# Inputs laid out ahead of the kernel and a new order of its instructions, in an attention and mixture-of-experts kernel

## The reference

```python
logits = jnp.einsum('bhqd,bhkd->bhqk', Q, K) + b[0]
logits = logits + -1e+30 * (1.0 - mask)
weights = jax.nn.softmax(logits, axis=-1)
out = jnp.einsum('bhqk,bhkd->bhqd', weights, V)
```

## Time and profile before

| what | value |
|---|---|
| median of three runs | 539.66 us |
| the profiled execution, its own time | 538.97 us |
| its span, first to last instruction | 537.2 us |
| mean granted TensorE clock | 0.982 |
| TensorE busy | 497.7 us (93%) |
| VectorE busy | 433.1 us (81%) |
| GpSimd busy | 364.5 us (68%) |
| ScalarE busy | 356.7 us (66%) |

### The profile page before, as it was taken

One profiled execution on the slowest core, in us unless ns is written; L12 is line 12 of the kernel. 1 busy time (PEld: TensorE's weight loads), 2 busy tenths in 40 slices (PEclk: granted clock), 3 DMA queues, 4 the chain that ended last, 5 costly groups with the idle time before them and its releaser, 6 DMA issues.

```text
span 537.2 us, 15110 instructions
## 1 busy us (share of the span) xinstructions
PE 497.7 (93%) x5549; PEld 324.0 (60%) x5549; DVE 433.1 (81%) x1404; ACT 356.7 (66%) x761; POOL 364.5 (68%) x633
## 2 busy tenths in 40 slices
PE   1756999999999999999999999999999999999893
PEld 1645565666656565766666566666666666655551
DVE  4735868899897979888897979799887785867897
ACT  3398698887967867677686866777566665655410
POOL 7644444588858869686868778686845857654865
PEclk9987899999999999999999999999999999999997
DMA  7402101010310101010110101000000000100010
GB/s 170 101 4 55 32 16 56 2 51 6 82 36 18 34 22 51 23 50 21 31 43 21 52 1 51 21 21 27 3 21 1 2 22 1 33 1 21 1 31 29
DMA packets 28503, 16.98 MB, mean 32 GB/s; under 512 B 3687, under 2 KB 28429, under 8 KB 28430
## 3 DMA queue, kind: packets, MB, share of 16 engines
q1 hardware_dynamic: 26670, 15.57, 10.5%
q10 hardware_dynamic: 1760, 0.46, 0.4%
HBM read 11.74 MB, written 4.24 MB: 30 GB/s over the span
## 4 chain that ended last, share of the span: by engine, by line
PE 64%; DVE 5%; issue 1%; ACT 0%; DVEq 0%
PE ps L2186 16%; PE ps L2134 16%; PE ps L2145 4%; PE ps L2079 4%; PE ps L2022 4%; PE ps L2096 4%; PE ps L2127 4%; PE ps L2164 2%; PE ps L2165 2%; PE ps L2104 2%; PE ps L2054 2%; PE ps L2177 2%; DVE weighed L1046 1%; PE ps L2083 1%; PE ps L2047 1%
## 5 line engine op out<-in xcount | busy, mean ns | idle before, releaser
L2186 PE MATMUL ps<-w_moeT,y4T 128*128 128x512 f32 x256 | 123.5, 607 | 1.2 <-DVE gd L1005 1.1
L613 POOL TENSOR_TENSOR sum<-weighed 128x512 f32<-128x512 f32 x60 | 76.1, 1269 | 71.2 <-DVE weighed L1046 71.2
L2134 PE MATMUL ps<-h,w 128*128 128x512 f16 x512 | 118.6, 379 | 0.0
L1638 ACT ACTIVATE h<-ps 128x512 f16<-128x512 f32 x128 | 74.1, 591 | 46.9 <-PE ps L2134 35.9
L1046 DVE TENSOR_TENSOR weighed<-ps,wgt 128x1024 f32<-128x1024 f32 x64 | 77.8, 1218 | 31.7 <-PE ps L2186 30.7
L969 DVE SCALAR_TENSOR_TENSOR h<-ps,h 128x512 f16<-128x512 f32 x128 | 85.6, 682 | 20.2 <-ACT h L1638 20.1
L2134 PEld LDWEIGHTS ps<-h,w 128*128 128x128 f16 x512 | 48.3, 98 | 56.2 <-issue 5.6
L1604 ACT ACTIVATE prT<-ps,maskT 77x1024 f32<-77x1024 f32 x64 | 67.3, 1101 | 14.8 <-PE ps L2083 14.5
L2186 PEld LDWEIGHTS ps<-w_moeT,y4T 128*128 128x128 f32 x256 | 45.1, 189 | 43.0 <-issue 35.0
L565 POOL TENSOR_TENSOR rs<-ve,neg_half 128x4 f32<-128x4 f32 x64 | 64.9, 1013 | 8.7
L560 POOL TENSOR_TENSOR ve<-mv,eps 128x4 f32<-128x4 f32 x64 | 14.2, 222 | 60.6 <-DVE mv L903 60.4
(11 more groups left out here) (171 smaller groups left out, 986.1 us busy)
## 6 DMA issues: line engine op xcount, KB each, us to landing
cx<-in_ctx SPq DMA_DIRECT2D x16, 308.0 KB
xa<-in_x SPq DMA_DIRECT2D x16, 256.0 KB, 3.0
out_x<-xo SPq DMA_DIRECT2D x16, 256.0 KB, 2.3
plugs<-plug_d SPq DMA_DIRECT2D x16, 77.0 KB
nat<-in_L_ffn_W SPq DMA_DIRECT2D x1, 512.0 KB
k_u<-in_L_ffn_k ACTq DMA_DIRECT2D x1, 256.0 KB, 3.9
k_u<-in_L_ffn_k ACTq DMA_DIRECT2D x1, 128.0 KB, 3.4
k_u<-in_L_ffn_k ACTq DMA_DIRECT2D x1, 64.0 KB, 4.6
```

The costliest lines, as they stand in the source:

```text
L613: nc.gpsimd.tensor_tensor(sum4[:], both[:, 0:4 * D], both[:, 4 * D:8 * D], ALU.add).then_inc(c_sum4.sem, 1)
L1638: last = nc.scalar.activation(h[:, 0, (k - 1) % FC, :], src, ACT.Relu)
L2134: last = pe.matmul(pb(g, k), w2[:, i, c * 128:(c + 1) * 128], h1[:, g.p, part, i, :], start=(i == 0 and part == 0), stop=(i == FC - 1 and ...
L2186: last = pe.matmul(pm(g, j)[:, half, :], y4T[:, g.p, j * S:(j + 1) * S], w_moeT[:, half * 512:(half + 1) * 512], start=True, stop=True)
```

## The change

The order of the calls is new on all five engines, and the host-side function `kernel()` lays the inputs out before the launch, in a new function `laid_out`: only reshapes, transposes, copies, zeros and ones. The kernel's own arithmetic stays on the chip.

- The keys arrive turned and already spread with zeros for every other head (`kT`, 308 KB a group), the values with their column of ones (`vx`, 308 KB a group). `a_turn_keys`, `a_keys`, `a_values_in` and `make_values` are gone. The context is still loaded for the patches. `x` and the output are arranged so that each partition has one contiguous row of 2 KB a group.
- The experts' weights, `W_in` and the gate arrive turned, in one tile, with a second copy that repeats the last row; GpSimd subtracts it in place (`make_sums_zero`). `turn_weights`, `take_weights` and the turn of the mask are gone; the turned mask is loaded.
- The Boolean inputs come in one transfer and the scales in another, issued by ScalarE after `a_normalise(g[0])`. `make_weights` moves from ScalarE to VectorE.
- Two of the mask's four rows are sent from ScalarE's queue, ahead of its first work.
- The normalisations of groups 1 to 3 in stage a, and half of the third norm of group 15, are on VectorE.
- The sums at the end: group 14 has j = 1 and 3, group 15 j = 2 and 3 on VectorE, now as eight dependent multiply-and-add steps of 128 columns straight from PSUM (`e_accumulate`); group 15's j = 1 is weighed by ScalarE and summed by nine matmuls with the unit matrix (`e_sum`), and copied out (`e_take`). `keep_busy` is gone.

```diff
 SyncE:
             def load_keys(g):
+                if g.has(2):
+                    sp.wait_ge(a_less[1].sem, a_less[1].of(g, back=2))
+                sp.dma_start(kT[:, g.p], keys[g.n]).then_inc(keys_in[g.p].sem, 16)
+            def load_values(g):
+                if g.has(2):
+                    sp.wait_ge(a_pv.sem, a_pv.of(g, back=2))
+                sp.dma_start(vx[:, g.p], values[g.n]).then_inc(values_in[g.p].sem, 16)
...
             def mask_rows():
                 sp.wait_ge(made_mask, 1)
-                for r in range(R):
+                for r in range(R // 2):
                     sp.dma_start(mask_b[32 * r:32 * r + 1, :], mask0_b[:]).then_inc(masks_in, 16)
...
             load_rows(g[0])
-            load_masks()
+            load_mask()
+            load_lens()
+            load_context(g[0])
             load_rows(g[1])
             load_keys(g[0])
             mask_rows()
+            load_context(g[1])
+            load_values(g[0])
             load_keys(g[1])
...
+            load_values(g[14])
+            load_keys(g[14])
+            store(g[8])
+            load_values(g[15])
+            store(g[9])
+            plug(g[13])
             load_keys(g[15])
 VectorE:
+            def make_weights():
+                dve.wait_ge(made_s, 6)
+                dve.wait_ge(made_halves, 1)
+                nc.vector.tensor_scalar(w1[:], k0_d[:], s_sgn[:, 7:8], None, ALU.mult)
+                nc.vector.tensor_scalar(w2[:], k1_u[:], s_sgn[:, 5:6], s_sgn[:, 6:7], ALU.mult, ALU.add)
+                nc.vector.tensor_scalar(w3[:], k2_u[:], 2.0, -1.0, ALU.mult, ALU.add).then_inc(made_ffn, 1)
...
+            def a_normalise(g):
+                dve.wait_ge(ln_a.rs.sem, ln_a.rs.of(g))
...
+                for j in range(G):
+                    last = nc.vector.tensor_scalar(xn[0][:, g.p, j * D:(j + 1) * D], xa[:, g.f, j * D:(j + 1) * D],
+                                                   mv[0][:, g.p, j, 0:1], rs[0][:, g.p, j:j + 1], ALU.subtract, ALU.mult)
+                last.then_inc(a_xn_v.sem, 1)
...
+            def e_accumulate(g, j, half):
...
+                for e in range(4 * half, 4 * half + 4):
+                    so_far = xo if e else xd
+                    if e:
+                        dve.wait_ge(v_step.sem, v_steps(g, j) + e)
+                    last = nc.vector.scalar_tensor_tensor(xo[:, g.p, cols], pm(g, j)[:, e // 4, (e % 4) * D:(e % 4 + 1) * D],
+                                                          wgt[:, g.p, j, e:e + 1], so_far[:, g.p, cols], ALU.mult, ALU.add)
+                    last.then_inc(v_step.sem if e < E - 1 else c_weighed.sem, 1)
...
+            a_highest(g[1], 0)
+            make_weights()
+            a_stats(g[2])
+            make_plug()
+            a_stats(g[3])
+            a_highest(g[1], 1)
+            a_normalise(g[2])
+            a_split_maxima(g[1])
+            a_normalise(g[3])
             a_weigh(g[0])
...
+            e_weigh(g[15], 0)
+            e_accumulate(g[15], 2, 0)
+            e_accumulate(g[15], 2, 1)
+            e_accumulate(g[15], 3, 0)
+            e_accumulate(g[15], 3, 1)
 ScalarE:
+            def mask_rows():
+                act.wait_ge(made_mask, 1)
+                for r in range(R // 2, R):
+                    act.dma_start(mask_b[32 * r:32 * r + 1, :], mask0_b[:]).then_inc(masks_in, 16)
...
+            def e_weigh(g, j):
...
+                for e in range(E):
+                    last = nc.scalar.activation(weighed[:, place(g, j), e * D:(e + 1) * D],
+                                                pm(g, j)[:, e // 4, (e % 4) * D:(e % 4 + 1) * D], ACT.Copy,
+                                                scale=wgt[:, g.p, j, e:e + 1])
+                last.then_inc(s_weighed.sem, 1)
...
+            mask_rows()
+            a_normalise(g[0])
             load_signs()
-            a_normalise(g[0])
-            a_keys(g[0])
             a_queries(g[0])
...
             a_exponent(g[1], 0)
+            b_normalise(g[0])
+            a_exponent(g[1], 1)
+            b_high(g[0], 0)
 TensorE:
+            def e_sum(g, j, *readers):
...
+                for e in range(E):
+                    pe.matmul(dst, ident[:], weighed[:, place(g, j), e * D:(e + 1) * D], start=(e == 0), stop=False)
+                pe.matmul(dst, ident[:], xd[:, g.p, j * D:(j + 1) * D], start=False, stop=True).then_inc(s_sum.sem, 1)
...
-            a_turn_keys(g[0])
             turn_ends()
             a_turn_rows(g[0])
             a_scores(g[0], 0)
+            a_turn_rows(g[1])
+            a_scores(g[0], 1, (a_max[0], g[0]))
             count_ends((s_ends, g[0]))
...
             a_scores(g[2], 1, (a_max[0], g[2]))
             b_turns(g[0], (a_prT[1], g[1]))
...
+            e_experts(g[13], 1, (a_prT[1], g[15]))
+            b_last(g[15])
             e_experts(g[13], 2, (c_weighed, g[13], 1))
-            b_last(g[15])
```

```diff
             e_experts(g[7], 2, (c_weighed, g[7], 2))
-            a_turn_rows(g[12], (a_prT[1], g[10]))
             a_turn_out(g[10])
             b_layer(g[9], 3)
             c_turns(g[8], (c_weighed, g[7], 3))
+            a_turn_rows(g[12], (a_prT[1], g[10]))
             b_layer(g[9], 4)
             a_turn_maxima(g[11], (a_att, g[10]))
-            a_turn_keys(g[12])
             c_project(g[8])
             a_scores(g[12], 0, (a_mT, g[11]))
             b_layer(g[9], 5)
+            e_experts(g[7], 3, (c_x3, g[8]), (c_yT, g[8]))
             b_layer(g[9], 6)
-            e_experts(g[7], 3, (c_x3, g[8]), (c_yT, g[8]))
```

More of the change, by code:

```diff
@@ L60, in turned_at, with build @@
         return self.turned.of(g, self.k, back)
[L63 to L68, removed]
-    G = 4
-    NG = B // G
+def build(nc, x, ctx, keys, values, mask, mask_turned, lens, b_attn, signs, scales, weights, biases, gains, patch_gains, out):
+    B, NK = mask.shape
+    G = 4
+    NG, S, D = x.shape[0], x.shape[1], x.shape[2] // G
+    DC = ctx.shape[2] // G
+    FC = 4
+    F = FC * D
+    assert signs.shape[1] == (2 + FC) * F + FC * D
+    E = weights.shape[2] // D - 1
     HD = D // HEADS
@@ new lines, in count, with place, place_free @@
+        def count(kind, g, j):
+            return sum(1 for i, k in sums_of if how(i)[k] in kind and (i.n, k) <= (g.n, j))
+        def place(g, j):
+            return buffered.index((g.n, j)) % 2
+        def place_free(g, j):
+            n, k = buffered[buffered.index((g.n, j)) - 2]
+            if how(Group(n))[k] == "scalar":
+                return s_sum.sem, s_sum.of(Group(n), k + 1)
+            return c_sum4.sem, added(Group(n), k)
+        def added(g, j):
+            return count(("gpsimd",), g, j)
@@ new lines, in v_steps, with __init__, of @@
+        def v_steps(g, j):
+            return (count(("vector",), g, j) - 1) * (E - 1)
+        class Counted(Signal):
+            def __init__(self, sem, kinds):
+                self.sem, self.kinds = sem, kinds
+            def of(self, g, k=None, back=0):
+                return count(self.kinds, Group(g.n - back), (G if k is None else k) - 1)
+        c_weighed = Counted(c_weighed.sem, ("gpsimd", "vector"))
+        s_weighed, s_sum, s_out = [Counted(s.sem, ("scalar",)) for s in (s_weighed, s_sum, s_out)]
@@ L360, in bcast, with shared, by_vector, normalised @@
+        def shared(ln, g):
+            return g.n == NG - 1 and ln.n == 2
+        def by_vector(ln, g):
+            return ln.n == 0 and 1 <= g.n <= 3
+        def normalised(ln, g, back=0):
+            i = Group(g.n - back)
+            if by_vector(ln, i):
+                return a_xn_v.sem, i.n
+            return ln.xn.sem, i.n + 1 - (3 if ln.n == 0 and i.n > 3 else 0)
         def bcast(ap, n):
@@ new lines, in normalise_rest @@
+            def normalise_rest(ln, g, src):
+                n, p = ln.n, g.p
+                dve.wait_ge(ln.rs.sem, ln.rs.of(g))
+                dve.wait_ge(ln.turned.sem, ln.turned_at(g, back=2))
+                for j in range(2, G):
+                    last = nc.vector.tensor_scalar(xn[n][:, p, j * D:(j + 1) * D], src[:, j * D:(j + 1) * D],
+                                                   mv[n][:, p, j, 0:1], rs[n][:, p, j:j + 1], ALU.subtract, ALU.mult)
+                last.then_inc(ln_rest[n].sem, 1)
@@ L2577, in _ @@
             e_experts(g[12], 0, (c_gd, g[12]))
-            a_values(g[15])
+            a_weights(g[15], 1, (a_prT[0], g[15]))
             b_layer(g[14], 1)
```

1412 lines of the change are left out of this document (747 added, 665 removed).

## The result

The changed kernel takes 548.39 us (median of 4 runs, 548.23 to 549.41), the kernel before, beside it on the same chip, 540.30 us. The ratio is 1.0154, with a 95% interval of 1.0132 to 1.0175: it is 8.1 us slower, where the prediction had 525 us, faster. The profiled execution took 548.42 us, its span is 546.6.

What follows compares the result with a forecast made beforehand. TensorE was taken to bound the middle, its idleness lying at both ends. From 538.97 us, front -4.5, middle -3.6 and tail -6.0 gave 524.9, stated as 525; own range 521 to 529, with rivals' bounds 518 to 532.

Steps and rivals of the forecast that it cites:

- Keys, context and rows ahead in the ring are 1.2 MB: Front: assumed these loads do not push the mask's rows later; they land near 10.7 us.
- the first scores: Front: start at 10.7 us instead of 13.65, -2.9 us, with bounds of -3.4 and 0.
- the third: Middle: SyncE's in-order issue delays key loads, TensorE waits at every `a_scores(g, 0)`; 551 us; chance 0.04.
- the first feed-forward turn: Front: `b_turns(g[0])` at 45.6 us against 50.08, -4.5 us, with bounds of 0 and -8.
- the first rival: Front: VectorE and GpSimd hold each other up, taking the 4.5 us back; 529.4, near 530 us; chance 0.2.
- its normalisations: Front: three normalisations moved to VectorE, 4 x 0.2 = 0.8 us each, 2.4 us together.
- the transposes: Middle: dropping the key transposes saves TensorE 0.30 us a group, 12 x 0.30 = 3.6 us (3.2 to 5.2).
- the moved expert pair: Tail: `e_experts(g[13], 2)`, 1.72 us, now comes behind T instead of ahead, so T is 1.7 us earlier.
- The rest of the order is shuffled by a place or two per period: Middle: between 0 and a few tenths of a us per period either way, taken as nothing.
- the fourth rival: Middle: TensorE's freed 0.3 us becomes idle because order changes cost as much; 528.5 us; chance 0.1.
- A dependent step of 128x128 out of PSUM: Tail: 0.32 us for each of VectorE's 16 last sum steps, 5.1 us.
- the first weighing: Tail: group 15's first weighing comes 21.7 us behind T instead of 22.8.

Runs made afterwards that it cites:

- the kernel with 128 rows: Changed kernel with the biases laid into row 127 of the turned weights, one load of 128 rows replacing 127 rows plus a biases transfer: 534.28 us, ratio 0.9902.
- the one experiment on it: Against the 128-row version, group 14's last slice weighed by VectorE in one instruction and summed by GpSimd: 532.2 us, ratio 0.9863.

## Why the prediction was wrong

The three stages of the prediction, in us of the profiled executions. T is where TensorE starts what follows the last layer of group 15; in the kernel with 128 rows:

```profile
45.26 0.66 PE L2217 MATMUL ps<-ident,xn 128*128 128x128 f32 x4 [2.03 <-ACT prT L1750]
```
```profile
495.24 1.94 PE L2379 MATMUL ps<-w_T,y4T 128*128 128x512 f32 x4
```

| Stage | before | forecast | changed | 128 rows, 531.22 us | 128 rows, 535.0 us |
|---|---|---|---|---|---|
| to `b_turns(g[0])` | 50.1 | 45.6 | 61.3 | 45.3 | 45.4 |
| from there to T | 451.9 | 446.6 | 451.5 | 450.0 | 452.0 |
| T to the end | 35.2 | 30.9 | 33.8 | 33.8 | 35.0 |
| span | 537.2 | 523.1 | 546.6 | 529.0 | 532.4 |

Of the 23.5 us between the forecast span and the changed kernel's, 15.7 lie in the front, 4.9 in the middle and 2.9 in the tail.

**The step that failed** stands in the front: "Keys, context and rows ahead in the ring are 1.2 MB, more than the rows had before; that this does not push them later is an assumption." It was applied to the mask rows alone, and there it held. The transfers behind it, the new weight load ahead of group 2's rows above all, were not priced at all: the sum from the first scores to `b_turns(g[0])` has no term for group 2's rows. That load cost 16.1 us of the front against a forecast that was otherwise 0.3 us off. None of the four rivals had it; the third, "the keys come late", had the right kind of mechanism (a load held up by what stands ahead) at the wrong place. The range ended at 532.

By the Trainium skill (DMA: Bandwidth & Descriptors, section "Why a DMA increments its semaphore by 16 and not by 1") a transfer is spread over the largest number of engines, at most 16, that divides the slowest dimension of both sides: 128 rows over 16 engines, 127, a prime, over one. The traces agree: 0.06 to 0.07 of the engines' time at 26 to 28 GB/s from 32 to 38 us with 127 rows, and with 128 the same load landed 9.3 us after its issue. The rule could have been weighed against the code of the change, in which the number of rows stands.

**The front's other steps came out, in part by luck.** The first scores (10.64) and that the last mask row releases them were right, and the first feed-forward turn with 128 rows is near (45.26 for 45.6). But VectorE's work is part of what bounds the front now, as the first rival said: its normalisations took 2.13 and 1.11 us where 0.8 was reckoned. Four times the row named for them, 0.28 us, is 1.12 and not 0.8; and 2.13 is the one beside GpSimd. Giving two of them back brought 1.7 us at the first feed-forward turn. The forecast met the time since other terms erred the other way: the values came 1.6 us earlier than reckoned, and VectorE made the three weights in 2.1 us instead of 3.1. The turn of 1.1 us "at the slow clock of the start" is the length of such a turn in the kernel before (11.85 us, 1.11); the granted clock reads 1.00 there, so the reason given for it is not shown.

**The middle: the transposes were priced nearly right, the order was not.** TensorE's busy time from `b_turns(g[0])` to T fell by 4.9 us; 1.7 of it is the moved expert pair, and the 3.2 that are left are 0.24 for each of 13 groups, where 0.30 was forecast. The period says the same. By the last layers of groups 7 and 8 in the kernel before and with 128 rows it went from 29.92 to 29.69 us, 0.23 less:

```profile
279.12 1.95 PE L2145 MATMUL ps<-w,h 128*128 128x128 f16 x32
...
309.04 1.95 PE L2145 MATMUL ps<-w,h 128*128 128x128 f16 x32
```
```profile
274.02 1.95 PE L2335 MATMUL ps<-w,h 128*128 128x128 f16 x32
...
303.71 1.95 PE L2335 MATMUL ps<-w,h 128*128 128x128 f16 x32
```

The prediction's period of 30.15 us is 0.2 too long: it was taken between two turns of the maxima, and the key transposes stand behind the first and ahead of the second.

TensorE's idle time in that stage rose from 5.6 to 8.6 us, though. "The rest of the order is shuffled by a place or two per period ... taken as nothing" is the step that failed here: one place on VectorE, made long by GpSimd, is a wait of 2.3 us (a second one 1.3), and where the clock falls behind it 2 us more. That is near the fourth rival, to which 0.1 was given; but the loss lies at two places and not in every period. From `b_turns(g[0])` on, TensorE never waited for the loads of keys and values.

**The tail: two terms were undersized.** A dependent step of 128x128 out of PSUM is 0.38 us (seven take 2.67), not 0.32, for which the nearest row of another instruction stood: 16 of them are 1.0 us more. And the first weighing comes 23.8 us behind T, not 21.7. With 128 rows VectorE is at work from 508.2 us, without a break worth naming, to that weighing at 519.03; two slices of group 14 at three us each stand in this stretch, of which I had reckoned half a slice. That they bound the stage is read from the timeline; the one experiment on it moved the work into GpSimd's way and does not prove it. The store's 2.6 us for 2.9 gives 0.3 back.

**Medians and profiled executions.** The forecast sat on an execution with the clock at full level in the middle. Of the eleven executions of the kernel with 128 rows eight took 534.1 us or more, and of their two profiles the longer one has both drops: 2.0 us in the middle and 1.3 in the tail. That the other seven have them too is a reading of their times.

## What to carry to other kernels

Read the number of rows of each new transfer before its bytes: take the last row along, or cut the transfer (112 + 15 and 125 + 2 rows did as well as 128 here), and don't leave a row out of a large load for the sake of a bias. The slow transfer held back the loads of the other queue too, so price what is issued behind it, not only whom it feeds. Where a bounding engine has no idle time, a shuffle of the others' orders isn't free: look for the instruction that it waits for next, and at what GpSimd does in that moment.

## What was unexpected of the hardware

- One transfer of 575.5 KB over one engine, issued by ScalarE, held back what SyncE issued: a store of 32 KB landed 18.3 us after its issue, against 2.3 with 128 rows.
- Issued by SyncE, it kept that engine's sequencer 7.01 and 10.49 us in the two issues behind it, of 580 and of 4.5 KB; issued by ScalarE, the same two took 0.41 and 0.43 us, and the time was almost the same (546.95 and 548.39).
- VectorE instructions of 0.2 us took 0.43 to 1.21 us beside GpSimd sums, in the middle and in the tail. By the Trainium skill (SBUF — State Buffer, section "SBUF: two separate sides") the two share a port pair under an exclusive lock; the rows agree.
- Behind a wait of TensorE of 2.3 to 2.5 us the clock fell to 1.2 GHz for some 3 us in one profiled execution of the kernel with 128 rows and not in the other. The tail's clock fell or held as well, and not always together with it.
